# The gated experts of a decoder's last stage: fp32 products as one fp32 operation, or as three products of split operands held as fp32r

## The reference, cut to what matters

```python
x = inputs.reshape(-1, d)
gate_logits = jax.nn.softmax(x @ gate_w + gate_b, axis=-1)
selected = (gate_logits >= 0.1).astype(x.dtype)
weights = gate_logits * selected
weights = weights / jnp.where(wsum == 0, jnp.ones_like(wsum), wsum)   # wsum: the row's sum
for e in range(E):                                                    # E = 8
    out = out + weights[:, e:e + 1] * (x @ expert_w[e] + expert_b[e])
...
x = _layernorm(x + out)
```

## Time and profile before

| | us |
|---|---|
| median of 3 runs | 2374.05 |
| lowest, highest of them | 2367.06, 2374.99 |
| span of the profiled execution (first to last instruction) | 2359.6 |
| span of the last stage, from its first loads at 2059.9 | 299.7 |
| last stage's first expert product | 2079.2 |
| TensorE busy in the whole span | 1925.9 (82%) |
| DVE busy in the whole span | 1338.2 (57%) |
| mean granted TensorE clock, share of 2.4 GHz | 0.916 |

### The profile page before, as it was taken

The page is one execution under the profiler, slowest core; times in us unless marked ns, Lnnn a source line. Parts: engine busy times, 40 slices in busy tenths (PEclk is TensorE's granted clock), DMA queues, the critical chain, the costliest instruction groups (busy, mean ns, idle before and its releaser), DMA issues. The chain is left out here.

```text
span 2359.6 us, 30423 instructions
## 1 busy us (share of the span) xinstructions
PE 1925.9 (82%) x8687; PEld 1166.3 (49%) x8687; DVE 1338.2 (57%) x3285; ACT 943.9 (40%) x2525; POOL 625.2 (26%) x797
## 2 busy tenths in 40 slices
PE   6794857888888888838949999994665999689998
PEld 6453534454445545516635665652444666444443
DVE  1384438899898989834432222226772455546666
ACT  2232549888888988803312222211111323100000
POOL 1000005555555555503530000006542011100000
PEclk9997979999999999976669999997887999989999
DMA  7322741221221122031242213204332021110110
GB/s 267 103 103 89 257 163 45 59 64 51 62 63 44 60 62 63 18 105 55 90 144 68 80 63 107 71 27 139 109 98 83 32 83 64 46 45 27 36 36 18
DMA packets 173998, 188.55 MB, mean 80 GB/s; under 512 B 18596, under 2 KB 157083, under 8 KB 172864
## 3 DMA queue, kind: packets, MB, share of 16 engines
q1 hardware_dynamic: 166592, 162.76, 21.2%
q0 software_dynamic: 6144, 16.18, 2.0%
q10 hardware_dynamic: 1152, 8.39, 0.9%
HBM read 114.48 MB, written 67.11 MB: 77 GB/s over the span
## 5 line engine op out<-in xcount | busy, mean ns | idle before, releaser
L745 POOL TENSOR_SCALAR xa_probs<-xa_probs,xa_rinv 128x512 f32<-128x512 f32 x512 | 344.5, 692 | 294.9 <-DVE xa_rinv L790 294.9
L910 PE MATMUL xa_ps_t<-xa_ident,xa_probs 128*128 128x128 f32 x2048 | 325.7, 286 | 61.3 <-POOL xa_probs L745 55.3
L763 ACT ACTIVATE xa_probs<-xa_ps_s,xa_nmax 128x512 f32<-128x512 f32 x512 | 351.9, 708 | 25.5 <-DVE xa_nmax L794 25.1
L910 PEld LDWEIGHTS xa_ps_t<-xa_ident,xa_probs 128*128 128x128 f32 x2048 | 232.3, 143 | 240.6 <-POOL xa_probs L745 84.2
L794 DVE TENSOR_REDUCE xa_nmax<-xa_ps_s 128x2 f32<-128x1024 f32 x256 | 307.3, 1201 | 39.3 <-PE xa_ps_s L902 38.0
L680 ACT ACTIVATE xa_probT<-xa_ps_t 128x512 f32<-128x512 f32 x368 | 226.5, 621 | 63.5 <-PE xa_ps_t L910 54.4
L2340 PE MATMUL ga_ps_e<-ga_ew,ga_xT 128*128 128x512 f32 x512 | 235.0, 609 | 0.0
L902 PE MATMUL xa_ps_s<-xa_k,xa_q 96*128 96x512 bf16 x512 | 158.1, 391 | 54.2 <-ACT xa_probs L763 34.4
L2280 DVE SCALAR_TENSOR_TENSOR ga_acc<-ga_ps_e,ga_gate,ga_acc 128x256 f32<-128x256 f32 x256 | 123.9, 484 | 79.8 <-PE ga_ps_e L2340 71.7
L2340 PEld LDWEIGHTS ga_ps_e<-ga_ew,ga_xT 128*128 128x128 f32 x512 | 95.5, 194 | 114.0 <-issue 102.6
L1405 ACT ACTIVATE ex_hid<-ex_ps_g 128x512 f32<-128x512 f32 x64 | 38.3, 598 | 253.8 <-PE ex_ps_u L1458 253.8
(11 more groups left out here) (356 smaller groups left out, 3142.4 us busy)
## 6 DMA issues: line engine op xcount, KB each, us to landing
xa_q<-scratch_qk_parts SPq DMA_DIRECT2D x192, 64.0 KB, 2.2
xa_k<-scratch_qk_parts SPq DMA_DIRECT2D x192, 64.0 KB, 2.2
scratch_buf<-mix_zeros ACTq DMA_DIRECT2D x8, 1024.0 KB, 12.2
ex_x<-scratch_buf SPq DMA_DIRECT2D x16, 512.0 KB, 4.5
scratch_results<-ex_out SPq DMA_DIRECT2D x16, 512.0 KB, 3.1
mix_chunk<-in_L_mix_w SPq DMA_DIRECT2D x12, 512.0 KB, 3.5
scratch_qk_parts<-proj_partsq SPq DMA_DIRECT2D x8, 768.0 KB, 4.5
scratch_qk_parts<-proj_partsk SPq DMA_DIRECT2D x8, 768.0 KB, 5.9
```

The costliest lines, as they stand in the source:

```text
L745: ins = pool.tensor_scalar(probs[h % NP][:, t, :], probs[h % NP][:, t, :], rinv[h % 2][:, t:t + 1], 1.0, ALU.mult, ALU.mult)
L763: ins = act.activation(probs[h % NP][:, t, :], ps_s[j][:, t % 2, :], ACT.Exp, bias=nmax[h % 2][:, t:t + 1], accum_out=rsum[h % 2][:, t:t + 1])
L910: ins = pe.transpose(ps_t[t % 2][:, i * P:(i + 1) * P], probs[(h - 2) % NP][:, i, t * P:(t + 1) * P], ident[:, :])
```

## The change

Only the last stage is edited. Each fp32 operand is split in a rounded part ("h", written as fp32r by ACT's copy) and the exact remainder ("l", by a DVE subtraction, written as fp32r). A product x w becomes three accumulated products xl wh + xh wl + xh wh. This is done for the experts and for the logits, not for the transposes and the biases.

- x: ACT's copy from PSUM now writes `xTh` and raises `xh_up`; a new DVE operation at the head of `prepare` makes `xTl` = ps_t - xTh and raises `xT_up`, for which `logits` waits.
- expert weights: once, ACT makes `ewh` (two copies of 128 x 2048, behind its prepare(0, 0)), DVE makes `ewl` (two subtractions of 128 x 2048, behind its prepare(0, 0)), and the first body waits for both halves instead of for the load.
- gate weights: one small copy and one small subtraction ahead of the first logits.

```diff
+def products(xh, xl, wh, wl):
+
+    for h in range(DH):
+        for xp, wp in ((xl, wh), (xh, wl), (xh, wh)):
+            yield h, xp, wp
...
+        xTh, xTl = ([r.sb(f"{n}{u}", [P, DH, S], F32R) for u in range(2)] for n in ("xTh", "xTl"))
...
             def prepare(b, u):
                 act.wait_ge(t_up, b + 1)
                 wait(act, e_up, T * PAIRS * (b - 1))
-                act.activation(xT[u][:, :, :], ps_t[:, :, :], ACT.Copy).then_inc(xT_up, 1)
+                act.activation(xTh[u][:, :, :], ps_t[:, :, :], ACT.Copy).then_inc(xh_up, 1)
...
+            act.wait_ge(c_ld, 48)
+            act.activation(gwh[:, :, :], gw[:, :, :], ACT.Copy).then_inc(gl_up, 1)
             prepare(0, 0)
+            act.wait_ge(ew_ld, 16 * E)
+            for h in range(DH):
+                act.activation(ewh[:, h, :, :], ew[:, h, :, :], ACT.Copy).then_inc(wh_up, 1)
...
+                dve.wait_ge(xh_up, b + 1)
+                dve.tensor_tensor(xTl[u][:, :, :], ps_t[:, :, :], xTh[u][:, :, :], ALU.subtract).then_inc(xT_up, 1)
                 dve.wait_ge(lg_up, b + 1)
...
+            dve.wait_ge(gl_up, 1)
+            dve.tensor_tensor(gwl[:, :, :], gw[:, :, :], gwh[:, :, :], ALU.subtract).then_inc(gl_up, 1)
             prepare(0, 0)
+            for h in range(DH):
+                dve.wait_ge(wh_up, h + 1)
+                dve.tensor_tensor(ewl[:, h, :, :], ew[:, h, :, :], ewh[:, h, :, :], ALU.subtract).then_inc(wl_up, 1)
...
-                    for h in range(DH):
-                        ins = pe.matmul(ps_l[:, t, :], xT[u][:, h, t * P:(t + 1) * P], gw[:, h, :], start=(h == 0), stop=(h == DH - 1))
+                    for n, (h, xp, wp) in enumerate(products(xTh[u], xTl[u], gwh, gwl)):
+                        ins = pe.matmul(ps_l[:, t, :], xp[:, h, t * P:(t + 1) * P], wp[:, h, :], start=(n == 0), stop=(n == 3 * DH - 1))
...
             turn(0, 0, 0)
+            pe.wait_ge(gl_up, 2)
             logits(0, 0)
             turn_gates(0, 0)
-            pe.wait_ge(ew_ld, 16 * E)
+            pe.wait_ge(wl_up, DH)
...
-                        for h in range(DH):
-                            ins = pe.matmul(ps_e[e // 2][:, :, :].rearrange("p e d -> p (e d)"), xT[u][:, h, t * P:(t + 1) * P],
-                                            ew[:, h, e:e + 2, :].rearrange("p e d -> p (e d)"), start=(h == 0), stop=(h == DH - 1))
+                        for k, (h, xp, wp) in enumerate(products(xTh[u], xTl[u], ewh, ewl)):
+                            ins = pe.matmul(ps_e[e // 2][:, :, :].rearrange("p e d -> p (e d)"), xp[:, h, t * P:(t + 1) * P],
+                                            wp[:, h, e:e + 2, :].rearrange("p e d -> p (e d)"), start=(k == 0), stop=(k == 3 * DH - 1))
```

More of the change, by code:

```diff
@@ L6 @@
 F32 = mybir.dt.float32
+F32R = mybir.dt.float32r
 BF16 = mybir.dt.bfloat16
@@ L2142, in stage_gated @@
         x_in = [r.sb(f"x{u}", [P, T, D]) for u in range(2)]
-        xT = [r.sb(f"xT{u}", [P, DH, S]) for u in range(2)]
+        xTh, xTl = ([r.sb(f"{n}{u}", [P, DH, S], F32R) for u in range(2)] for n in ("xTh", "xTl"))
         ew = r.sb("ew", [P, DH, E, D])
         eb = r.sb("eb", [E, D])
+        ewh, ewl = (r.sb(n, [P, DH, E, D], F32R) for n in ("ewh", "ewl"))
         gw = r.sb("gw", [P, DH, E])
+        gwh, gwl = (r.sb(n, [P, DH, E], F32R) for n in ("gwh", "gwl"))
         gb = r.sb("gb", [P, E])
@@ L2163, in stage_gated @@
         ld, st = ([r.sem(f"{n}{u}") for u in range(2)] for n in ("ld", "st"))
-        t_up, xT_up, lg_up, ex_up, gate_up, gt_up, gT_up, e_up, e_free, b_up, acc_up, var_up, rstd_up, out_up, steps, wr_up = (r.sem(n) for n in
-            ("t_up", "xT_up", "lg_up", "ex_up", "gate_up", "gt_up", "gT_up", "e_up", "e_free", "b_up", "acc_up", "var_up", "rstd_up", "out_up", "steps", "wr_up"))
+        t_up, xT_up, lg_up, ex_up, gate_up, gt_up, gT_up, e_up, e_free, b_up, acc_up, var_up, rstd_up, out_up, steps, wr_up, xh_up, wh_up, wl_up, gl_up = (r.sem(n) for n in
+            ("t_up", "xT_up", "lg_up", "ex_up", "gate_up", "gt_up", "gT_up", "e_up", "e_free", "b_up", "acc_up", "var_up", "rstd_up", "out_up", "steps", "wr_up", "xh_up", "wh_up", "wl_up", "gl_up"))
         block = ctx.enter_context(nc.Block())
```

## The result

Slower by about 1%: 2398.31 us median (2393.57 to 2406.04, 4 runs) against 2372.18 (2367.06 to 2374.99, 4 runs); the ratio is 1.0101, 95% interval 1.0079 to 1.0123. The medians are 26.1 us apart. The forecast was 2388.9, slower by 14.8, in a range of 2365 to 2430.

The account below looks back on a forecast made before the run. It took TensorE's chain in the last stage as the bound, 33.75 us a batch. Start +9.5, batches 0 to 6 +3.7, second wait +8.4, batch 7 -6.8 made +14.8 on the median 2374.05: 2388.9 us, range 2365 to 2430.

Parts of the forecast that it names:

- A1: Last stage: fp32r products take one pass and the clock falls; 2388.9 us, from 2377.0 to 2400.8; chance 0.66.
- A3: Last stage: gate products of 8 columns stay at two records each; +51.7 us with more half clock, 2425.8; chance 0.12.
- A4: Last stage: an fp32r product costs an fp32 record, 0.43 us; +171.2 us, 2545; chance 0.10.
- A2: Last stage: the clock holds, or falls only while TensorE stands anyway; -9.0 us, 2365.0; chance 0.12.
- The expert products: TensorE, each batch: 96 one-pass products at 0.216 us take 20.7 us instead of 27.5, -6.8.
- The gate products: TensorE, each batch: eight products of two records become 24 of one; +0.93 us, +1.79 in the first.
- The new wait: Before the gate products: TensorE stands 3.0 us a batch for DVE's subtraction, queued behind tile 1's last multiply-add.
- The second wait: At tile 1, batches 1 to 7: TensorE waits for DVE's multiply-adds to free the first buffer, +1.2 us each.
- The start: Start of the last stage: subtractions, slower gate products and weight copies put the first bias product 9.5 us later.
- The clock: Behind each batch's standing and gate products: granted clock falls to half, costing 3.4 us, bounds 1.7 and 5.1.
- The sum: Whole span: start +9.5, batches 0 to 6 +3.7, waits at tile 1 +8.4, batch 7 -6.8; together +14.8 us.

Follow-up runs that it names:

- the early subtraction: Against the changed kernel, DVE's subtraction for x moved ahead of the multiply-adds of tile 1's third pair; ratio to the kernel before 0.9958, stage 285.7 us.

## Why the prediction was right, and where its sizes were off

**The case.** It forecast A1: one pass a product, one record, and a clock that falls. All three came. A3 (gate products at two records) and A4 (0.43 a record) are out by the record counts, A2 by the clock of 0.88.

**The expert products.** -6.8 a batch was -5.7: 96 x 0.227 = 21.8 for 27.5. This is the mis-sized term. The row chosen for the price, fp32 records of 256 columns, reads 0.22 by its sum and 0.216 as the most frequent distance from start to start, which the forecast took. Such a record streams as many columns behind one weight load as an fp32r record of 512, and yet it is quicker; no run shows why. The runs with bf16 parts show 0.011 us a record more for four-byte operands than for bf16. 96 x 0.011 x 8 makes 8.4 us, about the 8.7 by which the stage exceeded the forecast of 14.8; the other errors nearly cancel, and that is luck.

**The gate products.** +0.93 was +0.8 (24 records at 0.1115 for 16 in 1.85), one record each; from start to start 1.78 us became 2.67, +0.9.

**The new wait.** 3.0 was 2.23 to 2.31 a batch as idle time. The idle time counts from the modelled end of the last product; from start to start the gate products come 2.5 us later than in the kernel with the early subtraction, and their first record takes 0.1 more, 2.6 in all. The mechanism is shown by the early subtraction. The forecast was too long mainly because it took the start of the last multiply-adds from the old rows, 0.65 us behind the moment TensorE was ready (2164.95 and 2165.60 in the earlier trace rows); behind fp32r products it is some 0.3 (2223.73; the last expert record starts at 2223.22, so TensorE was ready at 2223.45).

**The second wait.** +1.2 came in three pieces, in the batch shown 0.31 and 0.34 for DVE and 0.38 for the load of x; together 1.0 of idle time, about 1.3 from start to start. The last piece had been missed, so that the size came out is partly luck: the prediction moved no load, but a shorter batch asks for it earlier. In the changed kernel it is issued at 2215.34, 0.6 us behind the store, and lands 4.4 us later, which is when the transposes start (2219.74).

**The start.** +9.5 was +9.3. ACT's copies took 3.69 (3.8 forecast), DVE's subtractions 4.49 together (4.6 forecast), and the walk through the chain held.

**The clock.** 3.4 us of loss a batch was 4.0 in the first profile: 37.0 less the 33.05 that batch 1 leaves when its one stretch (1.7) is taken off. Two to three stretches came in most batches; the upper bound of three was close to what came. Shown: with the wait filled, half of the half clock is gone, so standing and thin products together cost it. The gate products alone cost it in six of six batches there, in two of six with the early subtraction and in one of six (fp32, 1.85 us) in the kernel before. What decides from batch to batch is open, and so is whether two parts are always short enough.

**The sum.** Forecast: 9.5 + 10.9 for batches 0 to 6 - 5.6 for batch 7 = 14.8. Measured: 9.3 + 19.2 (260.4 for 241.2 us) - 4.9 = 23.5. Without the clock's fall the change would have been worth -0.7 us a batch (33.05 for 33.75), which the terms from start to start come near: -5.7 + 0.9 + 2.6 + 1.3 = -0.9; the gain of the expert products was used up by the wait first, and the clock turned it into a loss.

The direction and the mechanism were right. The size was little more than half: 14.8 forecast, 26.1 on the medians and 23.5 on the stage. The 2398.31 lies near the upper end of the likeliest case (2377 to 2401), where it got help from a measured time before that was 1.9 us below the one the forecast stood on.

## What to carry to other kernels

A faster product is worth what its surroundings let through: here -5.7 us a batch of product time met +2.6 of a wait that one DVE instruction in the wrong place made, and some 4 of clock behind it. When an operand gets a second part, look at who makes that part and what stands ahead of the maker in its own program, before counting passes. And look at what the granted clock does behind products of a few columns: here it fell there without a wait too, and streaming work put ahead of them gave half of the lost clock back.

## What the hardware showed beyond the forecast

- An fp32r record of 512 columns takes 0.227 us at the full clock, bf16 0.216; at the half clock both take 0.427. With 256 columns fp32r takes 0.120 and 0.213, with 8 columns 0.111 and 0.213: at the half clock 8 columns take as long as 256, so there the weight load sets the pace of the shorter ones.
- bf16 records of 8 columns follow at 0.026 us, fp32r ones at 0.111: the four-byte type keeps fp32's load time. The Trainium skill ("TensorE: Matmul & The Clock Gate", Weight-path perf modes) ties the fast weight load to an input type that is not fp32 and sees no win for fp32. The trace agrees for bf16 and puts fp32r on fp32's side (8-column fp32 records stand 0.112 apart).
- TensorE lost the full clock behind 1.9 us of 8-column products without a wait at them, in four of six batches of the kernel with fp32 gates, in one of six before the change, and in none of six when these were split in two parts of 0.9 us (one execution each).
- Filling a wait with products that nobody reads made the stage 14 us faster, and the ratio of the runs agrees: 1.0045 (1.0018 to 1.0073) for 1.0101 (1.0079 to 1.0123).
